# A routed mixture-of-experts block on one core: the late weight groups, the release of the output PSUM, the last block's halves and the last norm are rearranged

## The chip, the cores and the metric

The kernel runs on 1 core of one Trainium2 chip. The metric is the device time of one execution in microseconds, median of the runs shown. A profiled execution gives the trace.

## The reference

`x` has 16 batches of 256 rows of 256, the context 16 batches of 120 rows. What is computed, cut to what matters:

```python
x = x + xattn(layernorm(x), ctx, ctx)             # one head, softmax over 120 keys
h = layernorm(x)
logits = h @ Wr.T + br                            # 8 experts, the best 2 with softmax weights
for e in range(8):
    y = gelu(h @ W1[e].T + b1[e], approximate=False) @ W2[e].T + b2[e]     # 256 -> 1024 -> 256
    out = out + cw[:, e, None] * y
z = out + h
z = (z - mean(z)) * rsqrt(var(z) + 1e-12) * ln_w + ln_b
return x + z
```

## The kernel before, in words

Every engine has its own hand-written program; semaphores hold them together. The order of the work is therefore the order in which each engine's block calls its functions.

*First part (0 to about 184 us).* `steps` runs 16 batches, each taken through attention, routing and seat assignment in a pipeline of steps. Beside this the expert weights are turned: `transpose_group` (PE, L780) transposes four 128x128 tiles of `stage` into one of two PSUM banks `b_w`, `high_part` (ACT, L998) writes their high fp16 half, `low_part` (DVE, L1161) the rest. There are 64 such groups; PE may turn group n once n - 1 low parts are done (`wlo_ready`). The last 16 are late: eight of them run inside the last steps, and `late_groups(do, first, end)` calls the last eight, all of them W2, after the steps. All of W1 is done at `wlo_ready` = 56, everything at 64.

*Table.* After the steps DVE makes, from the counts in `b_rank` and the seats in `b_seats` (PSUM, last written by the matmuls L874), a list of 39 blocks of up to 256 rows: L1271 to L1321, with four small matmul steps of PE in between (L883 to L890, `table_ready`, `table_mm`). `blocks_ready` (L1317) says that expert and row of each block are known.

*Blocks.* For each block POOL's `fetch(m, p)` loads two registers, copies the indices (L633), starts a gather for each tile of 128 rows (L638) and copies the bias. PE's `turn` transposes the rows (L901), ACT's `x_high` (L1071) and DVE's `x_low` (L1328) split them into two fp16 parts, `up` does 48 matmuls (L922 to L924, four quarters in the PSUM banks 0 to 3), ACT's `gelu` (L1081) and DVE's `split` (L1337, L1339) make the two halves of h, and `down` does 48 matmuls (L944 to L946) into the banks 5 and 6, tile by tile within each of eight column parts. `y_out` on DVE evicts the two tiles (L1347), adds the norm's bias to a half batch of x1 (L1352) and multiplies by the gates (L1356), after which `y_ready` is raised. POOL's `give` copies the target indices (L650), once the earlier scatters have landed, waits for `y_ready` and scatters with addition into DRAM (L654). PE runs `up` of block j+1, `down` of j, `up` of j+2, `down` of j+1, and a `down` waits for `y_ready` of the block before:

```python
                j = 2 * m + p
                later = None
                at_least(pe, y_ready, j)
```

For the last block `up` lies before the previous block's `down`, so nothing is left to PE between the two.

*Early rows.* From m = 11 on, each pair of blocks also finishes a batch whose rows are complete: `measure_early` (DVE), `norm_early` (POOL), `normal_early` (ACT), `weigh_early` (POOL, L675), `finish_early` (DVE, L1387), which stands on DVE ahead of `y_out(m, 1)`.

*Last norm.* When all scatters have landed, SP loads the last eight batches; `measure_z` (DVE, L1421, L1425), `norm_pair` (POOL, L709 to L715), `normal` (ACT, L1121), `weigh` (POOL, L719; the last one DVE, L1440), `finish` (DVE, L1431) and `store` (ACT's queue, L1127) follow, two batches at a time. All of it is in place in `z_all`, in SBUF.

## Time and profile before

| what | us |
|---|---|
| median of 3 runs (663.43 to 664.11) | 664.06 |
| the profiled execution | 661.07 |
| its span | 659.4 |
| PE busy | 567.7 (86%) |
| DVE busy | 434.5 (66%) |
| ACT busy | 281.5 (43%) |
| POOL busy | 332.1 (50%) |
| DVE's block list finished (L1317, 192.99 + 0.17) | 193.16 |
| mean granted clock of TensorE | 0.938 of 2.4 GHz |

Times in the trace run from the span's start. A row of a timeline gives start, duration, engine, line, operation, written and read tiles, count, and in brackets how long the engine had been idle and what released it. In a row of stages each engine has its busy time and number of instructions; then come the clock (1.00 is 2.4 GHz, 0.50 is 1.2 GHz), the busy share of the DMA engines and GB/s. Matmuls are pipelined: their durations overlap, and their starts tell the pace.

### The profile page before, as it was taken

To read this page: it belongs to the slowest core of one execution; us is meant where nothing else is said; L and a number is where in the kernel's file an instruction comes from. 1 tells how busy PE (TensorE), PEld (TensorE's weight loads), DVE (VectorE), ACT (ScalarE), POOL (GpSimd) and SP (SyncE) were. 2 spreads that over 40 slices of the span, in tenths; PEclk is the share of its full clock that TensorE was granted. 3 is DMA by queue.
4 is the path that set the end of the run, shared out by engine and by line. 5 is a ranking of instruction groups with operands and counts; after the bars stand their busy time and mean duration, and the time that the engine had idled before them with its cause. 6 is when DMAs were issued, how large, how long until landed. Compare 5 with 4: busy or idle time off the path is not lost. (4 is left out here: it accounts for less than half of the span.)

```text
span 659.4 us, 17771 instructions
## 1 busy us (share of the span) xinstructions
PE 567.7 (86%) x4878; PEld 497.2 (75%) x4879; DVE 434.5 (66%) x1365; ACT 281.5 (43%) x699; POOL 332.1 (50%) x527
## 2 busy tenths in 40 slices
PE   5999888989647999998999999999999999999400
PEld 4888787887536887777989898988888898888300
DVE  2579988899874575446575656575667576666445
ACT  2687767666324333333333333325332433443022
POOL 4024433344313345544566666666766666665356
PEclk9999999888668999999999999999999999999855
DMA  7365665456432134332334342433434343443253
GB/s 217 100 190 194 187 208 170 156 168 197 126 93 55 35 50 62 58 66 55 58 59 64 57 64 57 64 73 76 85 74 91 68 82 88 89 80 59 41 144 127
DMA packets 62403, 65.71 MB, mean 100 GB/s; under 512 B 10088, under 2 KB 58032, under 8 KB 62352
## 3 DMA queue, kind: packets, MB, share of 16 engines
q1 hardware_dynamic: 46544, 44.10, 22.2%
q0 software_dynamic: 13632, 18.91, 18.6%
q10 hardware_dynamic: 2176, 2.10, 0.9%
q8 instruction: 22, 0.36, 0.2%
q14 instruction: 29, 0.24, 0.1%
HBM read 43.07 MB, written 22.02 MB: 99 GB/s over the span
## 5 line engine op out<-in xcount | busy, mean ns | idle before, releaser
L1081 ACT ACTIVATE stage<-bank,mt 128x256 f32<-128x256 f32 (+1 forms) x312 | 121.9, 452 | 138.9 <-PE bank L924 135.0
L922 PE MATMUL bank<-xnt,w1hi 128*128 128x256 f16 (+1 forms) x624 | 164.0, 264 | 9.0 <-DVE xnt L1328 5.5
L654 POOL DMA_INDIRECT sums_dram<-xn,mt x71 | 114.7, 1615 | 107.6 <-DVE xn L1356 89.9
L944 PE MATMUL bank<-w2hi,stage 128*128 x568 | 155.7, 274 | 10.9 <-DVE xn L1356 10.7
L923 PE MATMUL bank<-xnt,w1hi 128*128 128x256 f16 (+1 forms) x624 | 163.2, 263 | 0.0
L924 PE MATMUL bank<-xnt,w1lo 128*128 128x256 f16 (+1 forms) x624 | 163.2, 263 | 0.0
L946 PE MATMUL bank<-w2hi,stage 128*128 x568 | 155.5, 274 | 0.0
L945 PE MATMUL bank<-w2lo,stage 128*128 x568 | 155.5, 274 | 0.0
L1337 DVE CAST stage<-stage 128x512 f16<-128x512 f32 (+1 forms) x156 | 65.2, 418 | 115.0 <-PE bank L946 95.0
L638 POOL DMA_INDIRECT xg<-tokens_dram,mt x71 | 81.6, 1150 | 52.7 <-POOL mt L633 19.7
L1339 DVE TENSOR_TENSOR stage<-stage 128x512 f16<-128x512 f32 (+1 forms) x156 | 102.6, 657 | 5.4
L922 PEld LDWEIGHTS bank<-xnt,w1hi 128*128 x624 | 60.8, 97 | 22.6 <-issue 11.8
L944 PEld LDWEIGHTS bank<-w2hi,stage 128*128 128x128 f16 x568 | 55.7, 98 | 21.0 <-issue 14.9
L923 PEld LDWEIGHTS bank<-xnt,w1hi 128*128 x624 | 61.1, 98 | 5.8
L924 PEld LDWEIGHTS bank<-xnt,w1lo 128*128 x624 | 60.8, 97 | 6.1
L945 PEld LDWEIGHTS bank<-w2lo,stage 128*128 128x128 f16 x568 | 55.7, 98 | 6.6
L946 PEld LDWEIGHTS bank<-w2hi,stage 128*128 128x128 f16 x568 | 55.7, 98 | 6.5
L1071 ACT CAST xnt<-bank 128x512 f16<-128x512 f32 (+1 forms) x39 | 21.4, 548 | 67.2 <-PE bank L901 67.2
L780 PE MATMUL bank<-ident,stage 128*128 128x128 f32 x256 | 45.7, 314 | 4.2 <-DVE w2lo L1161 3.6
L586 POOL TENSOR_SCALAR nmu<-mv 128x4 f32<-128x4 f32 (+1 forms) x19 | 4.6, 242 | 88.6 <-DVE mv L1205 78.1
L780 PEld LDWEIGHTS bank<-ident,stage 128*128 128x128 f32 x256 | 36.0, 163 | 7.8 <-DVE w2lo L1161 3.5
L633 POOL COPY mt<-mt 128x2 int32 (+1 forms) x39 | 34.4, 883 | 5.9 <-DVE wvt L1321 4.8
(217 smaller groups left out, 915.4 us busy)
## 6 DMA issues: line engine op xcount, KB each, us to landing
stage<-in_L_ffn_W_dram SPq DMA_DIRECT2D x16, 768.0 KB, 4.9
work<-in_L_ffn_b_dram SPq DMA_DIRECT2D x39, 128.0 KB, 2.9
x<-in_x_dram SPq DMA_DIRECT2D x16, 256.0 KB, 5.1
tokens_dram<-xn SPq DMA_DIRECT2D x16, 256.0 KB, 2.2
sums_dram<-xn SPq DMA_DIRECT2D x16, 256.0 KB, 2.7
stage<-in_L_ffn_W_dram SPq DMA_DIRECT2D x16, 256.0 KB, 3.6
work<-sums_dram SPq DMA_DIRECT2D x8, 256.0 KB, 3.4
out_dram<-x SPq DMA_DIRECT2D x8, 256.0 KB, 3.2
```

The costliest lines, as they stand in the source:

```text
L638: nc.gpsimd.indirect_dma_start(out=xg[p][:, t, :], out_offset=None, in_=tokens_dram, in_offset=bass.IndirectOffsetOnAxis(ap=gidx[p][:, t:t ...
L654: nc.gpsimd.indirect_dma_start(out=sums_dram, out_offset=bass.IndirectOffsetOnAxis(ap=sidx[p][:, t:t + 1], axis=0), in_=y_sb[p][:, t, :], ...
L780: ins = nc.tensor.transpose(b_w[w][:, q * P:(q + 1) * P], stage[p][:, col:col + P], ident[:, :])
L922: nc.tensor.matmul(dst, w1hi[:, col], xhi[:, k, 0:bt], start=(k == 0), stop=False)
L923: nc.tensor.matmul(dst, w1hi[:, col], xlo[:, k, 0:bt], start=False, stop=False)
L924: ins = nc.tensor.matmul(dst, w1lo[:, col], xhi[:, k, 0:bt], start=False, stop=(k == KD - 1))
L944: nc.tensor.matmul(f_y[t], hhi[:, h], w2hi[:, col], start=(c == 0), stop=False)
L945: nc.tensor.matmul(f_y[t], hhi[:, h], w2lo[:, col], start=False, stop=False)
L946: ins = nc.tensor.matmul(f_y[t], hlo[:, h], w2hi[:, col], start=False, stop=(c == KF - 1))
L1081: ins = nc.scalar.activation(h32[:, c * bt:(c + 1) * bt], f_h[q][:, (c % 2) * bt:(c % 2 + 1) * bt], ACT.Gelu, bias=b1s[p][:, c:c + 1], sca ...
L1337: nc.vector.tensor_copy(hhi[:, s], h32[:, s]).then_inc(hhi_ready, 1)
L1339: nc.vector.tensor_tensor(hlo[:, s], h32[:, s], hhi[:, s], ALU.subtract).then_inc(split_ready, 1)
```

## The change

1. *Table and late groups.* DVE waits for the seats and makes the table before the low part of the group that the last step holds. PE turns one late group before the table's matmuls, three after them; the other four are turned inside `up` of block 0, one behind each quarter, and `up` needs only W1. `high_part` and `low_part` of these four go behind the four `gelu` and behind `x_low(0, 0)`. `fetch` reads the expert's register after its gathers are started.
2. *PSUM of outputs.* `down` waits for `y_self`, which the eviction raises. In `y_out` the gates are multiplied before the addition to x1.
3. *Last block.* `down` does all of tile 0, then all of tile 1. DVE evicts and multiplies each on its own, POOL scatters each on its own.
4. *Last norm.* `normal` writes into PSUM banks 0 to 7; DVE multiplies from there into `z_all`, POOL adds x1 (the last batch: DVE).

```diff
@@ fetch (POOL)
-                e = pool.value_load(eid[0:1, bass.ds(j, 1)], min_val=0, max_val=E - 1)
                 r = pool.value_load(row[0:1, bass.ds(j, 1)], min_val=0, max_val=UNITS - tb)
...
+                e = pool.value_load(eid[0:1, bass.ds(j, 1)], min_val=0, max_val=E - 1)
                 at_least(pool, gelu_ready, HB * (j - 1))
@@ give (POOL)
                 for t in range(tb):
+                    if isinstance(m, int) and j == BLOCKS - 1 and t > 0:
+                        alone(pool, y_ready, j + 1 + t, tally_pool)
@@ last norm (POOL)
-            def weigh(b):
...
+            def finish(b):
+                pool.wait_ge(zw_ready, b - ON_TIME + 1)
+                nc.gpsimd.tensor_tensor(z_all[:, b, :, :], z_all[:, b, :, :], x1[:, b, :, :], ALU.add).then_inc(o_ready, 1)
 
             norm_pair(0)
+            norm_pair(1)
+            for q in range(2, PAIRS):
                 norm_pair(q)
+                finish(ON_TIME + 2 * q - 4)
+                finish(ON_TIME + 2 * q - 3)
+            for b in range(NB - 4, NB - 1):
+                finish(b)
@@ PE
-            late_groups(transpose_group, 0, 2)
+            late_groups(transpose_group, 0, 1)
...
-            late_groups(transpose_group, 2, 8)
+            late_groups(transpose_group, 1, 4)
@@ up
                     if c % 2 == 1:
                         ins.then_inc(h_mm, 1)
+                        if beside is not None:
+                            beside(c // 2)
@@ down
-                at_least(pe, y_ready, j)
+                at_least(pe, y_self, j)
@@
             turn(0, 0)
+            pe.wait_ge(wlo_ready, GROUPS * NB + 4 * LATE - 8)
+            up(0, 0, weights_at(0, 0), (0, 1), beside=lambda q: late_groups(transpose_group, 4 + q, 5 + q))
+            turn(0, 1)
             pe.wait_ge(wlo_ready, GROUPS * NB + 4 * LATE)
@@ last block (PE)
-            down(LAST + 1, 0, weights_at(LAST + 1, 0))
+            at = weights_at(LAST + 1, 0)
+            j = BLOCKS - 1
+            pe.wait_ge(y_self, j)
+            pe.wait_ge(split_ready, HB * BLOCKS)
+            for t in range(TB):
+                for c in range(KF):
...
+                ins.then_inc(y_mm, HB // TB)
@@ ACT
-            ahead(0, 0, 0, 1)
+            for q in range(HB):
+                gelu(0, 0, q)
+                late_groups(high_part, 4 + q, 5 + q)
+            x_high(0, 1)
@@ normal (ACT)
-                    ins = nc.scalar.activation(z_all[:, b, j, :], z_all[:, b, j, :], ACT.Identity,
+                    ins = nc.scalar.activation(bank[b - ON_TIME][:, j * D:(j + 1) * D], z_all[:, b, j, :], ACT.Identity,
@@ step and table (DVE)
-                low_part(t, project, 3)
+                if not isinstance(t, int) or t < NB + 4:
+                    low_part(t, project, 3)
...
             dve.wait_ge(rank_kept, NB)
+            dve.wait_ge(seats_mm, NB)
...
-            late_groups(low_part, 0, 8)
+            low_part(NB + 4, None, 3)
+            late_groups(low_part, 0, 4)
@@ y_out (DVE): the gates' loop and its wait now stand ahead of this
                 if tiles(m, p) == TB:
@@ DVE
             keep_gate(0, 0)
+            late_groups(low_part, 4, 8)
             x_low(0, 1)
@@ last block (DVE)
-            y_out(BLOCKS // 2, 0)
...
+            for t in range(TB):
+                dve.wait_ge(y_mm, HB * last + HB // TB * (t + 1))
...
+                dve.wait_ge(y_self, last + t + 1)
@@ last norm (DVE)
-            def finish(b):
...
+            def weigh(b):
+                dve.wait_ge(zn_ready, b - ON_TIME + 1)
+                nc.vector.tensor_tensor(z_all[:, b, :, :], bank[b - ON_TIME][:, :].rearrange("p (j d) -> p j d", j=TJ),
+                                        lnw_bc[:, :].unsqueeze(1).to_broadcast([P, TJ, D]), ALU.mult).then_inc(zw_ready, 1)
```

PE's order from the seats to the table's last matmuls, before the change (L780 is `transpose_group`, four transposes of one group) and with it (L784):

```order
355 L874 MATMUL bank<-w2hi 128x256 [waits hot_ready]
356 L874 MATMUL bank<-w2hi 128x256 x3
357 L780 MATMUL bank<-ident,stage 128x128 [waits wlo_ready]
359 L780 MATMUL bank<-ident,stage 128x128 [waits wlo_ready,w_loaded0]
361 L780 MATMUL bank<-ident,stage 128x128 [waits wlo_ready]
363 L883 MATMUL bank<-work,before 128x2 [waits table_ready]
```

```order
355 L878 MATMUL bank<-w2hi 128x256 [waits hot_ready]
356 L878 MATMUL bank<-w2hi 128x256 x3
357 L784 MATMUL bank<-ident,stage 128x128 [waits wlo_ready]
359 L784 MATMUL bank<-ident,stage 128x128 [waits wlo_ready,w_loaded0]
361 L887 MATMUL bank<-work,before 128x2 [waits table_ready]
```

One group has moved behind the table's matmuls. Between these and `turn` stood six groups, now three.

DVE's order from the table's end to the second block's rows, before (L1161 is `low_part`, L1328 `x_low`) and with the change (L1185, L1354):

```order
405 L1321 TENSOR_TENSOR wvt<-work 128x272
406 L1161 SCALAR_TENSOR_TENSOR w2lo<-bank,w2hi 128x512 x8
407 L1328 TENSOR_TENSOR xnt<-bank,xnt 128x512
411 L1366 COPY mt<-xg 128x2
412 L1328 TENSOR_TENSOR xnt<-bank,xnt 128x512
```

```order
405 L1346 TENSOR_TENSOR wvt<-work 128x272
406 L1185 SCALAR_TENSOR_TENSOR w1lo<-bank,w1hi 128x512
407 L1185 SCALAR_TENSOR_TENSOR w2lo<-bank,w2hi 128x512 x4
408 L1354 TENSOR_TENSOR xnt<-bank,xnt 128x512
412 L1392 COPY mt<-xg 128x2
413 L1185 SCALAR_TENSOR_TENSOR w2lo<-bank,w2hi 128x512 x4
414 L1354 TENSOR_TENSOR xnt<-bank,xnt 128x512
```

Four low parts have moved between the first and the second `x_low`, and one of W1 from before the table to behind it.

POOL's order in the last norm, before (L719 multiplies by the weights) and with the change (L722 adds x1):

```order
674 L719 TENSOR_TENSOR w1hi<-w1hi,ctx_sb 128x512 x2
678 L715 TENSOR_TENSOR w1lo<-w1lo 128x4
679 L719 TENSOR_TENSOR w1hi<-w1hi,ctx_sb 128x512 x2
683 L715 TENSOR_TENSOR w1lo<-w1lo 128x4
684 L719 TENSOR_TENSOR w1hi<-w1hi,ctx_sb 128x512 x3
```

```order
677 L718 TENSOR_TENSOR w1lo<-w1lo 128x4
678 L722 TENSOR_TENSOR w1hi<-w1hi,x 128x512 x2
682 L718 TENSOR_TENSOR w1lo<-w1lo 128x4
683 L722 TENSOR_TENSOR w1hi<-w1hi,x 128x512 x5
```

POOL's seven operations of 512 columns stay seven, but begin after the third norm and are the last operation on each batch.

## Rows read from the trace of the kernel before

**Rows 1.** Stages: start:end, length, busy us (x count) of each engine, clock, DMA.
```profile
182.40:204.10 21.70, 10.10 (x47) 7.72 (x46) 14.97 (x53) 7.44 (x12) 5.50 (x11) 0.62 0.38 99
...
631.10:659.40 28.30, 0.00 (x0) 0.00 (x0) 16.11 (x41) 8.28 (x16) 17.30 (x23) 0.50 0.44 149
```

**Rows 2.** Timeline of DVE at the table: start, us, instruction [idle before <-releaser].
```profile
183.97 0.69 DVE L1161 SCALAR_TENSOR_TENSOR w1lo<-bank,w1hi 128x512 f16<-128x512 f32 x1 [2.01 <-ACT w1hi L998]
184.57 0.16 DVE L1271 COPY work<-bank 128x8 f32<-128x8 f32 x1
```

**Rows 3.** Timeline of PE from the last seats to block 1.
```profile
181.41 1.03 PE L874 MATMUL bank<-w2hi 128*128 128x256 f16 x4 [1.51 <-DVE w2hi L1224]
...
204.08 0.28 PE L922 MATMUL bank<-xnt,w1hi 128*128 128x256 f16 x1 [1.52 <-DVE xnt L1328]
...
209.33 0.60 PE L901 MATMUL bank<-ident,xg 128*128 128x128 f32 x4
211.70 0.28 PE L922 MATMUL bank<-xnt,w1hi 128*128 128x256 f16 x1 [1.77 <-DVE xnt L1328]
```

**Rows 4.** Timeline of POOL, the first index copy for a gather.
```profile
194.72 0.18 POOL L633 COPY mt<-mt 128x2 int32 x1 [4.81 <-DVE wvt L1321]
```

**Rows 5.** Stages of a quarter microsecond, PEclk before the busy share of DMA.
```profile
202.25:202.50 0.25, 0.25 (x2) 0.00 (x0) 0.11 (x1) 0.10 (x1) 0.00 (x0) 0.66 0.06 17
```

**Rows 6.** PE's waits in all (us, times, longest), then its timeline.
```profile
PE bank L944 <- DVE xn L1356: 10.7, 8, 5.0
...
457.81 0.28 PE L944 MATMUL bank<-w2hi,stage 128*128 x1 [0.72 <-DVE xn L1356]
...
616.13 0.39 PE L944 MATMUL bank<-w2hi,stage 128*128 x1 [5.02 <-DVE xn L1356]
...
618.67 0.37 PE L944 MATMUL bank<-w2hi,stage 128*128 x1
```

**Rows 7.** Timeline of DVE, then of POOL, one round with early rows.
```profile
501.52 0.75 DVE L1347 SCALAR_TENSOR_TENSOR xn<-bank,work 128x256 f32<-128x256 f32 x2
...
502.51 0.61 DVE L1356 TENSOR_SCALAR xn<-xn,mt 128x256 f32<-128x256 f32 x2
...
523.64 0.69 DVE L1387 TENSOR_TENSOR x<-x,work 128x512 f32<-128x512 f32 x1 [2.36 <-POOL work L675]
524.25 0.75 DVE L1347 SCALAR_TENSOR_TENSOR xn<-bank,work 128x256 f32<-128x256 f32 x2
...
503.97 1.63 POOL L654 DMA_INDIRECT sums_dram<-xn,mt  x1 [2.97 <-DVE xn L1356]
...
522.35 1.26 POOL L675 TENSOR_TENSOR work<-work,ctx_sb 128x512 f32<-128x512 f32 x1
```

**Rows 8.** Timeline of POOL, the scatters of the last two blocks.
```profile
618.67 1.56 POOL L654 DMA_INDIRECT sums_dram<-xn,mt  x1 [0.30 <-issue]
622.77 0.19 POOL L650 COPY mt<-wvt 128x2 int32 x1 [2.54 <-DMA sums_dram<-xn,mt]
...
627.22 1.55 POOL L654 DMA_INDIRECT sums_dram<-xn,mt  x1 [0.30 <-issue]
```

**Rows 9.** Timelines of POOL and of ACT's queue at the end, then four lines' durations.
```profile
635.76 0.25 POOL L709 TENSOR_SCALAR w1lo<-w1lo 128x4 f32<-128x4 f32 x1 [6.99 <-DVE w1lo L1425]
...
637.41 0.20 POOL L715 TENSOR_TENSOR w1lo<-w1lo 128x4 f32<-128x4 f32 x1
...
649.76 4.15 POOL L719 TENSOR_TENSOR w1hi<-w1hi,ctx_sb 128x512 f32<-128x512 f32 x3
...
654.49 2.19 ACTq L1127 DMA_DIRECT2D out_dram<-w1hi  x4
...
L1121 ACT ACTIVATE w1hi<-w1hi,w1lo x16: 585/586/602, 637.6 to 651.3; 128x256 f32<-128x256 f32 x16
L1431 DVE TENSOR_TENSOR w1hi<-w1hi,x x8: 677/679/1745, 640.9 to 655.6; 128x512 f32<-128x512 f32 x8
L1328 DVE TENSOR_TENSOR xnt<-bank,xnt x39: 417/683/694, 203.2 to 598.8; 128x512 f16<-128x512 f32 x32, 128x256 f16<-128x256 f32 x7
```

More of the change, by code:

```diff
@@ L359, in build @@
         o_ready = sem("o_ready")
+        last_done = sem("last_done")
         stored = sem("stored")
@@ L906, in weights_at, with up @@
                 return pe.value_load(woff[0:1, bass.ds(2 * m + p, 1)], min_val=0, max_val=(E - 1) * WE)
-            def up(m, p, at, after):
+            def up(m, p, at, after, beside=None):
                 j = 2 * m + p
@@ L1125, in store @@
             def store(b):
-                act.wait_ge(o_ready, b - ON_TIME + 1)
+                if b < NB - 1:
+                    act.wait_ge(o_ready, b - ON_TIME + 1)
+                else:
+                    act.wait_ge(last_done, 1)
                 act.dma_start(out_v[:, b, :, :], z_all[:, b, :, :]).then_inc(stored, 16)
@@ L1349, in y_out @@
                 ins.then_inc(y_self, 1)
+                dve.wait_ge(y_self, j + 1)
+                for t in range(tiles(m, p)):
+                    ins = nc.vector.tensor_scalar(y_sb[p][:, t, :], y_sb[p][:, t, :], gate_now[p][:, t:t + 1], None, ALU.mult)
+                ins.then_inc(y_ready, 1)
                 if tiles(m, p) == TB:
@@ L1353, in y_out @@
                                             x1[:, bass.ds(f, 1), half, :].rearrange("p a d -> p (a d)"), lnb_bc[:, :], ALU.add)
-                dve.wait_ge(y_self, j + 1)
-                for t in range(tiles(m, p)):
-                    ins = nc.vector.tensor_scalar(y_sb[p][:, t, :], y_sb[p][:, t, :], gate_now[p][:, t:t + 1], None, ALU.mult)
-                ins.then_inc(y_ready, 1)
                 if not (isinstance(m, int) and 2 * (m + 1) + p >= BLOCKS):
@@ L1413, in _ @@
                 blocks_of(m, m - ON_TIME_AT)
-            y_out(BLOCKS // 2, 0)
+            last = BLOCKS - 1
+            dve.wait_ge(b2_loaded[0], 16 * (last // 2 + 1))
+            dve.wait_ge(scattered[0], landed(last // 2, 0))
+            for t in range(TB):
+                dve.wait_ge(y_mm, HB * last + HB // TB * (t + 1))
+                nc.vector.scalar_tensor_tensor(out=y_sb[0][:, t, :], in0=f_y[t], scalar=1.0 / W_SCALE,
+                                               in1=b2_now[0], op0=ALU.mult, op1=ALU.add).then_inc(y_self, 1)
+                dve.wait_ge(y_self, last + t + 1)
+                nc.vector.tensor_scalar(y_sb[0][:, t, :], y_sb[0][:, t, :], gate_now[0][:, t:t + 1], None, ALU.mult).then_inc(y_ready, 1)
+            f = FULL - 1
+            nc.vector.tensor_tensor(x1[:, f // 2, f % 2, :], x1[:, f // 2, f % 2, :], lnb_bc[:, :], ALU.add)
             def measure_z(q):
@@ L1436, in _ @@
                 measure_z(q)
-                finish(ON_TIME + 2 * q - 4)
-                finish(ON_TIME + 2 * q - 3)
-            dve.wait_ge(zn_ready, NB - ON_TIME)
-            nc.vector.tensor_tensor(z_all[:, NB - 1, :, :], z_all[:, NB - 1, :, :],
-                                    lnw_bc[:, :].unsqueeze(1).to_broadcast([P, TJ, D]), ALU.mult).then_inc(z_self, 1)
-            for b in range(NB - 4, NB - 1):
-                finish(b)
-            dve.wait_ge(z_self, PAIRS + 1)
-            finish(NB - 1)
+                weigh(ON_TIME + 2 * q - 4)
+                weigh(ON_TIME + 2 * q - 3)
+            for b in range(NB - 4, NB):
+                weigh(b)
+            dve.wait_ge(zw_ready, NB - ON_TIME)
+            nc.vector.tensor_tensor(z_all[:, NB - 1, :, :], z_all[:, NB - 1, :, :], x1[:, NB - 1, :, :], ALU.add).then_inc(last_done, 1)
 _INS = ['x', 'ctx_1024', 'L0_xattn_Wq', 'L0_xattn_bq', 'L0_xattn_Wk', 'L0_xattn_bk', 'L0_xattn_Wv', 'L0_xattn_bv',
```

20 lines of the change are left out of this document (6 added, 14 removed).

## The prediction

> **What bounds the kernel now.** I read the table by stages first [rows 1]. TensorE (PE) is busy in almost all of the stage of blocks, and hardly at all in two places: the turn from routing to blocks (182.4 to 204.1 us: 10.1 of 21.7 us) and the final norm (631.1 to 659.4: nothing). In the first of them the order is: the seat matmuls L874, VectorE's (DVE) chain for the block table, GpSimd's (POOL) gathers, `turn`, `x_high`, `x_low`, and the first matmul of `up` at 204.08 [rows 2 to 4].
>
> Inside the blocks I read what PE waits for [rows 6]: 10.7 us on L1356, `y_ready`, in 8 waits. One is 5.0 us, before the last block; the other seven sum to 5.7 us, the first at 457.81 with 0.72. They lie in the rounds that also finish early rows. The timeline of one such round [rows 7] says why: POOL runs nearly without a gap from the scatter at 503.97 to the end of its weigh at 523.61, then DVE adds (523.64) and evicts the odd block (524.25), multiplies by the gates, and the next scatter may start. That circle lasts 524.25 - 501.52 = 22.73 us. PE's own work in it is 0.72 us less, so **POOL and DVE, not PE, set the pace of these rounds**.
>
> At the end [rows 8, 9] PE is done; what counts is the scatter that starts last (627.22), its landing, eight loads, and POOL's norms and multiplications, until 649.76 + 4.15 = 653.91; DVE's adds and ACT's last store issues follow, until 656.68.
>
> **The change, part by part.** A measurement here tells about 0.2%, 1.3 us.
>
> (a) *Table sooner.* DVE's chain starts at 184.57, behind a low part that waits for ScalarE (ACT) [rows 2]; it needs only the seat matmuls, over at 181.41 + 1.03 = 182.44 [rows 3]. It now starts near 182.5: 2.05 us sooner, the low part going behind it. POOL's first index copy starts at 194.72 [rows 4], after two register loads that I take at 0.7 us each (estimate: half of the 1.4 us between DVE's finished list, 193.16 in the table above, and that copy, with 0.15 for the start); one of them moves behind the gathers. The gathers so come up to 2.75 us sooner, and `turn` is no longer kept behind six groups of transposes but waits for its rows. Before: `turn` ended at 202.56, 1.52 us ahead of `up` [rows 3]. After: near 198.5, `up` near 200.1, some 4 us sooner.
>
> (b) *Four groups beside block 0.* They aren't gone. PE gets four times four transposes inside `up`, 0.45 us each time (estimate: the four of `turn` take 0.60 with the end of their pipeline [rows 3]), ACT four activations, DVE four low parts of 0.69 [rows 2], and `x_low(0,1)` is behind the last one. With PE at 2.4 GHz throughout, `up` of block 1 would start near 209.7 instead of 211.70 [rows 3]. But the granted clock rose to the upper level only at 202.3, in the dense stretch just ahead of `up` [rows 5]. Now `up` starts earlier and behind thinner work, so I expect its first matmuls at 1.2 GHz. The price is in the last block: 12 matmuls took 616.13 to 618.67, 0.212 us each [rows 6], against (211.70 - 204.08 - 1.77 - 0.60) / 48 = 0.109 us in block 0 [rows 3], where 0.60 is `turn`: 1.2 us. Gain at `up` of block 1: 2.0 - 1.2 = 0.8; I take **1.2 us** for the chance that it is warm sooner. Bounds: 0 (all given back) and 2.9. From there to 457 us PE is the bound, so it stays.
>
> (c) *PSUM free at eviction.* PE's wait ends with the eviction (`y_self`) and not with the gates. From 501.52 + 0.75 = 502.27 to 502.51 + 0.61 = 503.12 [rows 7] this is 0.85 us. Also the gates go ahead of the x1 add; the add is 0.33 us of chain, of which a dependent start takes back about 0.12, so `y_ready` comes 0.21 sooner. In the first of the eight rounds the wait of 0.72 vanishes. Then POOL's circle decides: 22.73 - 0.21 = 22.52 a round against PE's 22.01. After the six further rounds the next to last stop has gained 0.86 + 6 x 0.21 = **2.1 us**. Not 5.7: the waits get shorter, about 0.4 us each, they don't go. Bounds: 0.9 (only the wait's end moves) and 5.7 (all seven waits).
>
> (d) *Last block.* PE's 5.02 us wait gets 0.85 shorter, which buys nothing by itself: the new order has tile 0 finished 24 matmuls early, so POOL could scatter it early, but its index copy waits for the landing of block 37's scatter: 618.67 to 622.77 [rows 8], now 0.21 sooner. Then 622.56 + 0.19 + 0.85 = 623.6 for tile 0 (0.85 us is what a scatter takes to start, as from 503.12 to 503.97 [rows 7]), 1.57 + 0.30 later 625.5 for tile 1. Its data is there: PE restarts at 615.28 and ends 2.54 + 36 x 0.109 + 0.3 = 6.8 us later, near 622.1, DVE 0.9 after that. Today 627.22 [rows 8]: **1.7 us**. Bounds: 0.5, if a wait between the two scatters costs as much as today's 0.8 us before the first and the landing is slower, and 2.6.
>
> (e) *Final norm.* POOL has 4 norms of 1.85 (635.76 to 637.61) and 7 operations of 512 columns at 1.26 as before, but DVE multiplies out of PSUM, and POOL's additions are now the last step. POOL's serial chain: 635.76 + 4 x 1.85 + 7 x 1.26 = 652.0, plus 0.2 of waits and 0.4 of what the last three cost beside DVE (4.15 against 3.78) [rows 9]: 652.6. Two store issues of 0.44 end at 653.5; today the last four end at 656.68. Gain **3.1 us**. DVE's fourth measurement is no longer behind additions that waited for POOL, so nothing else is late: its multiplications end near 649.4. Cover: ACT writes into PSUM; no row shows such an activation; the nearest is L1121 itself, 0.586 [rows 9], and between half and one and a half of that, 16 of them stay ahead of POOL's 16.8 us. Bounds of (e): 0 and 4.
>
> DVE's multiplication with a PSUM input: L1328 has one, median 683 ns for 512 columns; L1431 has none, 679 alone [rows 9]. I take 0.68. The Trainium skill, "VectorE: DVE Perf Modes", section "The TRN2 errata — SBUF-src ops pay a fixed extra latency per instruction", speaks against the change: it gives a PSUM source 62 cycles more, an estimated 0.065 us at its 0.96 GHz. By that rule (e) would lose at most 8 x 0.065 = 0.5 us; by these rows nothing.
>
> **Sum:** 1.2 + 2.1 + 1.7 + 3.1 = 8.1 us. The profiled span 659.4 becomes 651.3. The profiled execution took 661.07, 1.7 more than its span; the median of the runs is 664.06, 3.0 above that. I take the gain off the median: **656.0 us**.
>
> **Rivals.**
> 1. *DVE and POOL still hinder each other in the norm.* L1431 took up to 1745 ns beside POOL, 677 alone [rows 9]: both have their inputs in SBUF. Now DVE has one input in PSUM and one in SBUF. If one is enough to collide, each of seven multiplications costs POOL up to 0.44 us, and gain (e) goes: 656.0 + 3.1 = 659.1. For: DVE's own weight row is still in SBUF. Against: L1328, with just such inputs, has a median of 683 and a maximum of 694 ns in the whole trace, POOL busy or not.
> 2. *The waits all go.* If POOL's gap-free stretch has slack that I don't see, (c) gives 5.7: 652.4. Against: [rows 7].
> 3. *The start gives nothing.* If the gates' store, and not the table, holds the gathers, or the clock stays low a little longer, (a) and (b) cancel: 657.2.
> 4. *Slower: the clock stays low.* PE starts `up` at 1.2 GHz with transposes and waits mixed in, and does not rise. Each matmul at the lower level costs 0.212 - 0.109 = 0.103 us. It takes (8.1 + 1.3) / 0.103 = 91 of them to make the kernel slower; through `up` 0, `up` 1 and `down` 0 (144) it is 14.8, of which (b) holds 1.2 already: about 656.0 + 14.8 - 1.2 = 669.6. Against: in the last block it rose after 12 matmuls.
>
> **Chances.** Forecast 0.70; rival 1 0.11; rival 2 0.06; rival 3 0.10; rival 4 0.03. All but the last, and a corner of 1 with 3 together, are faster by over 1.3 us: 0.94 faster, 0.03 same, 0.03 slower. The range holds rivals 1 and 3, and the low end takes (b) at 2.5 and (c) at 3 and (e) at 3.5: 653.0 to 660.0.
>
> **What would show it.** Start of the table chain near 182.5; first `up` near 200 at the lower clock, `up` of block 1 near 210.5 to 211; rounds of 22.5 us with a wait of 0.4 us on the eviction; last scatter to first scatter 1.9 us apart, released by no DVE row; POOL without a gap from the first norm to its last add, DVE's multiplications all below 0.7 us. A last add of POOL before 648 or after 651 us (652.6 less the 5.0 gained ahead of it is 647.6; a miss of 3) would make (e) wrong, an interval between odd evictions of 22.0 or 22.7 would make (c) wrong.

## The result and the profile after

| | before | changed |
|---|---|---|
| median of the runs (lowest to highest), us | 663.74 (660.65 to 664.11, 4 runs) | 652.88 (651.9 to 653.17, 4 runs) |
| profiled execution: time, span, us | 661.07, 659.4 | 651.9, 650.1 |
| granted TensorE clock, mean | 0.938 | 0.933 |

The changed kernel takes 0.9847 of the time before, 95% interval 0.9824 to 0.9871: 10.1 us less (8.6 to 11.7). The ratio weighs all runs and isn't the quotient of the two medians, which lie 10.9 apart; the gains of the parts alone, below, are taken from ratios too, differences between two changed kernels from medians. The forecast was 8.1 less. 652.88 lies just below the low end of the range, 653.0; the ratio applied to the 664.06 that the forecast started from gives 653.9, inside it.

The table chain and the first two blocks, timelines of DVE, then of PE, of the changed kernel, against [rows 2 and 3]:

```profile
179.84 0.17 DVE L1297 COPY work<-bank 128x8 f32<-128x8 f32 x1 [0.60 <-PE bank L878]
...
178.70 1.03 PE L878 MATMUL bank<-w2hi 128*128 128x256 f16 x4 [1.48 <-DVE w2hi L1248]
...
195.28 1.09 PE L905 MATMUL bank<-ident,xg 128*128 128x128 f32 x4 [1.60 <-DMA xg<-tokens_dram,mt]
197.85 0.39 PE L926 MATMUL bank<-xnt,w1hi 128*128 128x256 f16 x1 [1.48 <-DVE xnt L1354]
...
209.09 0.28 PE L926 MATMUL bank<-xnt,w1hi 128*128 128x256 f16 x1 [2.11 <-DVE xnt L1354]
```

Everything already stands 2.71 us earlier at the last seat matmuls (181.41 before, 178.70 now), in code that the change doesn't touch. So times are read from the seats, that is, from the start of the last four seat matmuls (L874, now L878). The table starts 0.11 us behind them, as forecast; `up` of block 0 comes 19.15 us behind them instead of 22.67; but `up` of block 1 comes 30.39 behind, where it was 30.29. The reason is in the stages of 1 us of the changed kernel, PEclk before the busy share of DMA:

```profile
199.00:200.00 1.00, 1.00 (x7) 0.69 (x6) 0.00 (x0) 0.00 (x0) 0.95 (x1) 0.50 0.00 0
200.00:201.00 1.00, 1.00 (x6) 0.94 (x5) 0.00 (x0) 0.37 (x2) 0.70 (x2) 0.50 0.27 55
201.00:202.00 1.00, 1.00 (x11) 0.91 (x10) 0.02 (x1) 0.95 (x3) 0.27 (x1) 0.98 0.29 97
```

`up` runs at 1.2 GHz for 3.2 us. The waits of PE in the blocks, then the last two on the timeline, against [rows 6]; the last line is the kernel before's counterpart of the first of these two:

```profile
PE bank L986 <- DVE xn L1373: 4.2, 1, 4.2
PE bank L950 <- DVE xn L1373: 3.8, 6, 1.6
...
590.07 0.28 PE L950 MATMUL bank<-w2hi,stage 128*128 x1 [0.44 <-DVE xn L1373]
610.56 0.35 PE L986 MATMUL bank<-w2hi,stage 128*128 x1 [4.16 <-DVE xn L1373]
...
594.79 0.28 PE L944 MATMUL bank<-w2hi,stage 128*128 x1 [0.74 <-DVE xn L1356]
```

Two evictions of odd blocks are 520.72 - 498.27 = 22.45 us apart (22.73 in [rows 7]), and POOL's multiplication (L678) is still what DVE waits for last ahead of them. DVE's timeline of the changed kernel:

```profile
498.27 0.75 DVE L1373 SCALAR_TENSOR_TENSOR xn<-bank,work 128x256 f32<-128x256 f32 x2
...
520.11 0.69 DVE L1413 TENSOR_TENSOR x<-x,work 128x512 f32<-128x512 f32 x1 [2.93 <-POOL work L678]
520.72 0.75 DVE L1373 SCALAR_TENSOR_TENSOR xn<-bank,work 128x256 f32<-128x256 f32 x2
```

The last block and the norm, POOL's timeline, ACT's queue, and two lines' durations (min/median/max), against [rows 8, 9]:

```profile
617.79 0.18 POOL L651 COPY mt<-wvt 128x2 int32 x1 [2.49 <-DMA sums_dram<-xn,mt]
...
620.67 1.55 POOL L657 DMA_INDIRECT sums_dram<-xn,mt  x1 [0.30 <-issue]
629.26 0.25 POOL L712 TENSOR_SCALAR w1lo<-w1lo 128x4 f32<-128x4 f32 x1 [7.04 <-DVE w1lo L1462]
...
639.03 6.59 POOL L722 TENSOR_TENSOR w1hi<-w1hi,x 128x512 f32<-128x512 f32 x5
...
641.55 5.01 ACTq L1151 DMA_DIRECT2D out_dram<-w1hi  x5
...
L1467 DVE TENSOR_TENSOR w1hi<-bank,ctx_sb x8: 656/680/692, 632.8 to 641.8; 128x512 f32<-128x512 f32 x8
L722 POOL TENSOR_TENSOR w1hi<-w1hi,x x7: 1255/1264/1710, 634.8 to 644.4; 128x512 f32<-128x512 f32 x7
```

Of POOL's seven adds one takes 1.71 us, the others 1.26. That one lies beside DVE's add of the last batch (L1479), the one operation of DVE there that has both inputs in SBUF.

In this pair of profiles the 9.3 us of the span are: setup and routing 2.7, which is not the change's; start of the blocks -0.1 (30.29 - 30.39); rounds 2.1 (594.79 - 590.07, less the 2.61 that `up` of block 1 had gained); last block 1.8 (627.22 - 620.67 = 6.55, less 4.72); norm 2.7 and 0.1 of rounding and loads. **The profiles give the change 6.5 us, the medians 10.1.** The experiments are about both numbers.

### The profile page after: what moved, and what is told of

It reads as the page before. It is cut to its first block, busy times and chain, and to the rows that moved or that the text cites. A ratio compares the mean times of both kernels' runs of the same rounds, so it can differ in the third digit from the quotient of the medians.

```text
span 650.1 us, 17773 instructions
## 1 busy us (share of the span) xinstructions
PE 564.9 (87%) x4878; PEld 496.0 (76%) x4879; DVE 431.6 (66%) x1365; ACT 279.5 (43%) x699; POOL 319.6 (49%) x527
## 4 chain that ended last, share of the span: by engine, by line
PE 43%; POOL 15%; issue 15%; DVE 11%; DMA 3%; POOLq 3%; ACT 2%; DVEq 1%; SPq 0%; ACTq 0%
PE bank L926 7%; PE bank L928 6%; PE bank L927 6%; PE bank L950 6%; PE bank L952 5%; PE bank L951 5%; POOL sums_dram L657 5%; POOL xg L638 2%; DVE st L1214 2%; PE bank L784 2%; PE bank L905 1%; POOL work L678 1%; POOL rn L590 1%; PE bank L865 1%; POOL w1hi L722 1%
## 5 line engine op out<-in xcount | busy, mean ns | idle before, releaser
L950 PE MATMUL bank<-w2hi,stage 128*128 x552 | 150.6, 273 | 4.0 <-DVE xn L1373 3.8
L951 PE MATMUL bank<-w2lo,stage 128*128 x552 | 150.5, 273 | 0.0
L952 PE MATMUL bank<-w2hi,stage 128*128 x552 | 150.5, 273 | 0.0
L638 POOL DMA_INDIRECT xg<-tokens_dram,mt x71 | 74.7, 1052 | 51.6 <-POOL mt L633 26.7
L950 PEld LDWEIGHTS bank<-w2hi,stage 128*128 128x128 f16 x552 | 53.9, 98 | 13.3 <-issue 7.5
L951 PEld LDWEIGHTS bank<-w2lo,stage 128*128 128x128 f16 x552 | 54.0, 98 | 6.1
L952 PEld LDWEIGHTS bank<-w2hi,stage 128*128 128x128 f16 x552 | 54.0, 98 | 6.0
L784 PE MATMUL bank<-ident,stage 128*128 128x128 f32 x256 | 44.6, 306 | 3.0 <-DVE w1lo L1185 2.4
L784 PEld LDWEIGHTS bank<-ident,stage 128*128 128x128 f32 x256 | 35.4, 160 | 5.6 <-DVE w1lo L1185 2.5
L633 POOL COPY mt<-mt 128x2 int32 (+1 forms) x39 | 31.1, 798 | 2.9 <-DVE wvt L1346 2.4
```

What stands on the lines that cost most here:

```text
L638: nc.gpsimd.indirect_dma_start(out=xg[p][:, t, :], out_offset=None, in_=tokens_dram, in_offset=bass.IndirectOffsetOnAxis(ap=gidx[p][:, t:t ...
L784: ins = nc.tensor.transpose(b_w[w][:, q * P:(q + 1) * P], stage[p][:, col:col + P], ident[:, :])
L950: nc.tensor.matmul(f_y[t], hhi[:, h], w2hi[:, col], start=(c == 0), stop=False)
L951: nc.tensor.matmul(f_y[t], hhi[:, h], w2lo[:, col], start=False, stop=False)
L952: ins = nc.tensor.matmul(f_y[t], hlo[:, h], w2hi[:, col], start=False, stop=(c == KF - 1))
```

## The experiments

All times that follow are medians beside runs of the kernel before on the same chip (its medians there: 662.9 to 663.6). The changed kernel itself was not run again beside them, so differences between these kernels and 652.88 under about 2 us are not told apart from none.

### The parts alone

**Only (e), the norm.** Of the change, this alone:

```diff
-                    ins = nc.scalar.activation(z_all[:, b, j, :], z_all[:, b, j, :], ACT.Identity,
+                    ins = nc.scalar.activation(bank[b - ON_TIME][:, j * D:(j + 1) * D], z_all[:, b, j, :], ACT.Identity,
```

with `weigh` on DVE and `finish` on POOL.

> The kernel before with the new last norm alone. Theory A (each part has a gain of its own, and 2.7 us of the 9.3 between the two profiled spans arose before the table, where nothing was changed): from the first load of the norm (28.3 us before the end of the span, 25.6 with the whole change) 25.6, so 2.7 us faster than before. Theory B (DVE and POOL still collide with one input of DVE in SBUF): POOL's seven additions stretch to 1.7 us each and the stretch stays at 28 us. First table of rows to look at: DVE's eight multiplications, 0.68 us each by A, up to 1.7 by B.

Measured: 659.55, ratio 0.9954 (0.9939 to 0.9968), 3.1 us less. From the first load of sums to the end it took 25.7 us, before 28.3.

**Only (c) and (d), release and halves.**

```diff
-                at_least(pe, y_ready, j)
+                at_least(pe, y_self, j)
```

with the gates ahead of the x1 add, and the last `down` tile by tile.

> The kernel before with the wait on the eviction, the gates ahead of the x1 addition, and the last block by halves; start and norm as before. Theory A: rounds of 22.5 us with waits of 0.45 us on the eviction, none in the first; last scatter 1.8 us sooner relative to the last block: 3.9 us faster. Rival (the 2.1 us of the rounds depend on the earlier start): waits of 0.7 us stay, 1.8 us faster.

Measured: 658.02, ratio 0.9912 (0.9895 to 0.993), 5.8 us less (4.6 to 7.0). The rounds are the changed kernel's, with waits of 0.45.

**Only (a) and (b), the start.**

```diff
-            up(0, 0, weights_at(0, 0), (0, 1))
+            up(0, 0, weights_at(0, 0), (0, 1), beside=lambda q: late_groups(transpose_group, 4 + q, 5 + q))
```

with the sooner table and gathers.

> The kernel before with the sooner table and the four late groups beside block 0 alone. Theory A: the shift of 2.6 us at the start of block 1 between the two profiles came from the setup, where narrow fp32 matmuls took 0.13 us each instead of 0.23; from the first of the last seat matmuls to the first matmul of block 1 it stays 30.3 us, and the kernel is 0 to 0.5 us faster than before. Theory C (the start itself gives the 2.6): that stretch is 27.7 us in this run and it is 2.6 us faster.

Measured: 661.43, ratio 0.9979 (0.9963 to 0.9994), 1.4 us less. `up` of block 1 starts 30.35 us behind the seats, so nothing is gained there by this profile. This profile also has two stretches of 1.2 GHz in the blocks, behind a wait of 2.00 us at 307 us and behind one of 2.15 us at 549.5.

The three ratios multiply to 0.9954 x 0.9912 x 0.9979 = 0.9846, and the whole change has 0.9847: within these intervals the parts don't disturb or help each other.

### The start: four groups beside block 0, and TensorE's clock

The level is TensorE's granted clock, 1.2 or 2.4 GHz; a fall is its change from 2.4 to 1.2. A fill is a row of matmuls on constants, placed where TensorE would wait; nothing reads what they write.

**The groups back ahead of block 0**, the sooner table kept:

```diff
-            late_groups(transpose_group, 1, 4)
+            late_groups(transpose_group, 1, 8)
```

> The changed kernel with all late groups turned before block 0 again, the table still sooner. Theory A: the sooner table pays by itself: up of block 0 starts after 7 groups of transposes that begin 2.0 us sooner than before, so from the last seat matmuls to block 1 it takes 28.3 us or less, and the four groups beside a slow block 0 cost what they gain: this kernel is 1 to 2 us faster than the changed one. Theory D (the groups beside block 0 pay as meant): 1 to 2 us slower than the changed kernel.

Measured: 653.77, ratio 0.9859 (0.9842 to 0.9876); intervals overlap with the changed kernel's, so neither theory's 1 to 2 us is borne out. Three timelines of PE, the last seats, the two `up`: this kernel, then the one with only (e), then the one with (c) and (d). The last two have the old start unchanged.

```profile
178.67 1.03 PE L878 MATMUL bank<-w2hi 128*128 128x256 f16 x4 [1.47 <-DVE w2hi L1242]
...
201.55 0.39 PE L926 MATMUL bank<-xnt,w1hi 128*128 128x256 f16 x1 [1.50 <-DVE xnt L1348]
...
210.67 0.28 PE L926 MATMUL bank<-xnt,w1hi 128*128 128x256 f16 x1 [1.78 <-DVE xnt L1348]
```
```profile
180.23 1.04 PE L876 MATMUL bank<-w2hi 128*128 128x256 f16 x4 [1.52 <-DVE w2hi L1229]
202.94 0.39 PE L924 MATMUL bank<-xnt,w1hi 128*128 128x256 f16 x1 [1.51 <-DVE xnt L1333]
...
212.24 0.28 PE L924 MATMUL bank<-xnt,w1hi 128*128 128x256 f16 x1 [1.78 <-DVE xnt L1333]
```
```profile
180.88 1.03 PE L876 MATMUL bank<-w2hi 128*128 128x256 f16 x4 [1.47 <-DVE w2hi L1237]
203.59 0.28 PE L924 MATMUL bank<-xnt,w1hi 128*128 128x256 f16 x1 [1.52 <-DVE xnt L1341]
...
211.21 0.28 PE L924 MATMUL bank<-xnt,w1hi 128*128 128x256 f16 x1 [1.78 <-DVE xnt L1341]
```

A first matmul of 0.39 is one at 1.2 GHz, 0.28 one at 2.4. The same start code gave both: 9.30 us between the two `up` at the lower level, 7.62 at the upper, so 1.7 us hang on a level that differs from one execution to the next. Seen from the seats, `up` of block 1 comes after 32.0 us (both kernels that began low without groups beside), 30.3 (high), and 30.3 to 30.5 with the groups beside block 0, which began low each time in the seven profiles without constant matmuls ahead of it. The sooner table alone moves nothing: `up` of block 0 comes 22.88 us behind the seats with it and 22.71 without. With the groups beside it, block 0 takes 11.24 us between the two `up`, without them 9.12: they cost 2.1 and save 3.7.

**TensorE busy ahead of the setup's matmuls.**

```diff
+            pe.wait_ge(pool_self, 1)
+            for i in range(34):
+                nc.tensor.matmul(bank[6][:, 0:P], ones_bf[:, :], ones_bf[:, :], start=True, stop=True)
```

> The changed kernel, with 34 bf16 128x128 matmuls of a constant into an unused PSUM bank while TensorE waits for the first weights; nothing reads them. Theory A (what the setup gains from run to run is TensorE's clock at the fp32 matmuls of one column: 1.05, 1.03 and 0.58 us for 8, 8 and 4 in one profile, 1.87, 1.84 and 0.99 in another, the same code): with the engine busy ahead of them they take 1.05, 1.03 and 0.58 us, the first V is evicted near 17.8 us, and the time is 0 to 2 us below that of the changed kernel, 651 to 653 us. Theory B (the difference comes from elsewhere, a transfer or a wait): they keep either time whatever ran before, and the time is 652.9 us or some tenths above, by what the extra matmuls delay.

Measured: 653.23, ratio 0.9862 (0.9834 to 0.989): not to be told from the changed kernel. This is the setup's first group of narrow matmuls in this kernel, and in the kernel of the run with two filled waits, below, which has that code as in the kernel before. Below them stand two stages of 1 us within that group, of the kernel before and of the changed one:

```profile
9.20 1.05 PE L759 MATMUL bank<-bqk,w2lo 128*128 128x1 f32 x8 [0.32 <-DVE w2hi L1179]
```
```profile
11.16 1.86 PE L756 MATMUL bank<-bqk,w2lo 128*128 128x1 f32 x8
```
```profile
11.00:12.00 1.00, 1.00 (x6) 1.00 (x6) 0.00 (x0) 0.20 (x2) 0.85 (x3) 1.00 1.10 351
11.00:12.00 1.00, 1.00 (x12) 1.00 (x11) 0.00 (x0) 0.04 (x1) 0.92 (x2) 1.00 1.12 356
```

Of 12 profiles without this fill (with before and after) eight show 1.05 to 1.08 and four 1.86 to 1.87; the last seats came at 178.4 to 179.5 us in the former and at 180.2 to 181.8 in the latter. The kernels before, only (e), and (c) with (d) were of the latter, the changed one of the former. The stages show 6 matmuls in a microsecond against 12 and a clock of 1.00 in both, so that this is TensorE's clock is not shown. Nor is it shown that it is a toss: it was slow in all three profiles of kernels without the sooner table, and in one of the nine with it. Both profiles with the fill have the fast one, which eight of twelve have without it. The fill brought this group 1.3 us forward against the changed kernel (9.20 against 10.51) and the seats to 178.1; the median doesn't show it.

**TensorE busy ahead of `up` of block 0**, then **also ahead of `up` of block 1** (the last two lines):

```diff
+            for _ in range(20):
+                nc.tensor.matmul(bank[3][:, 0:P], ones_bf[:, :], ones_bf[:, :], start=True, stop=True)
             late_groups(transpose_group, 1, 4)
...
             turn(0, 1)
+            for _ in range(28):
+                nc.tensor.matmul(bank[7][:, 0:P], ones_bf[:, :], ones_bf[:, :], start=True, stop=True)
```

> The changed kernel, with constant bf16 128x128 matmuls in TensorE's idle stretches ahead of the first block: 20 behind the block list, 18 behind the late groups that come before the block, 11 behind its turn. Nothing reads them. Theory A (the changed start gains nothing because up of block 0 begins at 1.2 GHz: 0.213 us per matmul for its first 3 us): up of block 0 starts at 2.4 GHz, 0.107 us per matmul, up of block 1 starts 28.7 to 29.3 us behind the last seat matmuls, where the changed kernel has 30.4, and the time is 1.1 to 1.7 us below that of the changed kernel, near 651.5. Theory B (what follows up of block 0 waits for something else, the gather of block 1 or the splits of the late groups): up of block 0 is shorter, but up of block 1 stays at 30.4 and the time at 652.9. Theory C (the extra matmuls delay the late groups or the turn more than they save): over 653.5.

Measured: 653.54, ratio 0.9855 (0.9825 to 0.9885). `up` of block 0 began at 2.4 GHz and `up` of block 1 28.15 us behind the seats, 2.2 us sooner than in the changed kernel. Then it was given back. PE's timeline of this kernel:

```profile
207.62 0.28 PE L930 MATMUL bank<-xnt,w1hi 128*128 128x256 f16 x1 [2.11 <-DVE xnt L1360]
...
208.94 0.39 PE L930 MATMUL bank<-xnt,w1hi 128*128 128x256 f16 x1
209.13 0.42 PE L931 MATMUL bank<-xnt,w1hi 128*128 128x256 f16 x1
```

Behind the wait of 2.11 us the level fell, at 208.9, and rose again at 212.2. The same wait, of 2.10 to 2.20 us, had no fall behind it in the seven other profiles that have it. None of the three theories had this.

> The changed kernel with constant matmuls ahead of the first block as in the run before (20, 18 and 11), and 28 more in the 2.1 us that TensorE waits between the turn of block 1 and its up, in another bank. Theory A (the first warm start was given back because the granted clock fell to 1.2 GHz behind that wait, from 208.9 to 212.2 us, 16 matmuls at 0.213 us): with the wait filled the clock stays at 2.4 GHz through up of block 1, the Fori's first wait (296.6 in the changed kernel, seats + 117.9) comes 1.8 to 2.3 us sooner relative to the last seat matmuls, and the time is 1.5 to 2.3 us below that of the changed kernel, near 651. Theory B (the clock falls somewhere later in the block, whatever fills the first waits): the same 653 to 653.6 as with the first warm start.

Measured: 650.94, ratio 0.9826 (0.9795 to 0.9857), six runs from 648.64 to 655.38. That is 1.9 us below the changed kernel, as theory A has it, but the intervals overlap. The wait was down to 0.58 and the level stayed. The profiled run is one of the long ones: slow setup (above), and another fall, behind a wait of 2.00 us ahead of `up` of block 12:

```profile
308.00:309.00 1.00, 0.33 (x2) 0.26 (x3) 0.97 (x3) 0.00 (x0) 0.00 (x0) 0.87 0.00 0
309.00:310.00 1.00, 1.00 (x7) 0.68 (x5) 0.97 (x3) 0.00 (x0) 0.00 (x0) 0.50 0.00 0
310.00:312.00 2.00, 2.00 (x11) 1.38 (x10) 1.49 (x4) 0.57 (x2) 0.00 (x0) 0.50 0.00 0
```

From that `up` to the wait near 478 us it is 171.31 us here and 169.64 in the changed kernel's profile, which has no fall there: 1.7 us. The wait of 2.00 us ahead of block 12 is in all 13 profiles in which it isn't filled, the fall in 7 of them.

### The rounds

**Gates behind the x1 add again**, PSUM still free at the eviction:

```diff
-                for t in range(tiles(m, p)):
-                    ins = nc.vector.tensor_scalar(y_sb[p][:, t, :], ..., gate_now[p][:, t:t + 1], None, ALU.mult)
-                ins.then_inc(y_ready, 1)
                 if tiles(m, p) == TB:
                     ...
+                (the same lines here)
```

> The changed kernel with one thing put back: VectorE multiplies a block's outputs by their gates behind the x split of the block that follows, and not at once behind the eviction. PSUM is still free at the eviction. Theory A (with PSUM free at the eviction, the rounds are set by the circle of the gates, the scatter and the index copies of VectorE and GpSimd): gates that come later make the scatters later, the rounds go from 22.45 us to 22.6 to 22.7 and the last ones with them; 1.0 to 1.7 us slower than the changed kernel, 653.9 to 654.6. Theory B (the release of PSUM alone is worth the gain; the order of the gates doesn't matter, since the scatter has a whole round to land): rounds of 22.45 us and 652.6 to 653.2.

(The gates stood behind the x1 add, not behind the x split as the expectation says; the place is that of the kernel before.)

Measured: 660.78, ratio 0.997 (0.9948 to 0.9992); one more execution took 1292.4 us, for no reason that the runs show. 7.9 us slower than the changed kernel, many times what both theories said. PE's waits, two evictions of odd blocks on DVE, and POOL's timeline at a round's first scatters:

```profile
PE bank L950 <- DVE xn L1373: 9.7, 6, 1.6
...
502.41 0.74 DVE L1373 SCALAR_TENSOR_TENSOR xn<-bank,work 128x256 f32<-128x256 f32 x2
526.06 0.75 DVE L1373 SCALAR_TENSOR_TENSOR xn<-bank,work 128x256 f32<-128x256 f32 x2
```
```profile
504.85 1.63 POOL L657 DMA_INDIRECT sums_dram<-xn,mt  x1 [2.97 <-DVE xn L1382]
506.79 2.08 POOL L657 DMA_INDIRECT sums_dram<-xn,mt  x1 [0.30 <-issue]
508.31 1.04 POOL L633 COPY mt<-mt 128x2 int32 x1
```

and the same three in the changed kernel:

```profile
500.51 1.63 POOL L657 DMA_INDIRECT sums_dram<-xn,mt  x1 [2.76 <-DVE xn L1378]
502.45 1.56 POOL L657 DMA_INDIRECT sums_dram<-xn,mt  x1 [0.30 <-issue]
503.46 0.80 POOL L633 COPY mt<-mt 128x2 int32 x1
```

Rounds are 23.65 us, 1.2 more than in the changed kernel and 0.9 more than in the kernel before, which has the same order but the later release. The later gates are 0.2 us of the 1.2; the rest goes with POOL being slower at the same work: from 470 to 590 us its scatters take 1.87 us in the mean, in the changed kernel 1.65, its index copies 1.20 and 0.93. They now lie at other places beside DVE's instructions. Beside the scatter of 2.08 us is this one of `split`'s casts, which elsewhere take 0.43:

```profile
507.95 0.65 DVE L1363 CAST stage<-stage 128x512 f16<-128x512 f32 x1
```

So the two seem to hinder each other, as DVE and POOL do in [rows 9]. This is the likeliest reading and not shown: scatters of 1.56 us have such casts beside them too, and no run moved one.

**TensorE waits for the gates again**, the gates still first:

```diff
-                at_least(pe, y_self, j)
+                at_least(pe, y_ready, j)
```

> The changed kernel with the other half of its part on PSUM undone: TensorE waits for the gates (the count behind the multiplication) and not for the eviction, but the gates still stand ahead of the x1 add. So it keeps what the run with gates last gave up, and gives up what that one kept. Theory A (GpSimd's circle sets the rounds, and what makes it short is that gates and scatter come early): rounds of 22.45 us as in the changed kernel, TensorE's wait in them 0.9 to 1.2 us in place of 0.45 and paid once, at the last of them; 0 to 0.9 us slower than the changed kernel, 652.9 to 653.8. Theory B (TensorE that starts later shifts VectorE's splits against GpSimd's scatters and makes them collide, as the run with gates last showed: scatters of 1.87 us in place of 1.65): rounds of 22.7 to 23.7 us and 654.5 to 661.

Measured: 653.8, ratio 0.9874 (0.9851 to 0.9898), 0.9 us over the changed kernel, which is within the noise. Rounds of 22.54 us with waits of 0.53. So the order of gates and add is nearly all of part (c): 22.73 to 22.54 by it, 22.54 to 22.45 by the earlier release; and the release without the order is a loss (rounds of 23.65 against 22.73).

**The early rows' multiplication on DVE.**

```diff
-                pool.wait_ge(early_zn, i + 1)
-                nc.gpsimd.tensor_tensor(z_now[i % 2], z_now[i % 2], lnw_bc..., ALU.mult).then_inc(early_zw, 1)
...
+                dve.wait_ge(early_zn, i + 1)
+                nc.vector.tensor_tensor(z_now[i % 2], z_now[i % 2], lnw_bc..., ALU.mult).then_inc(early_zw, 1)
                 dve.wait_ge(early_zw, i + 1)
```

> The changed kernel with one operation moved, in the rounds that also finish early rows: the multiplication of 512 columns by the norm's weight goes from GpSimd (1.26 us a round) to VectorE, just ahead of the add that waited for it. Theory A (GpSimd's circle of 22.45 us is what is left between the rounds and TensorE's 22.0): GpSimd has 1.26 us less, the circle opens, TensorE's seven waits of 0.45 us go, the one near 545 (1.3 to 1.6 us in most profiles) shrinks, rounds are 22.0 us; VectorE has 2.7 us of idle time in the round and takes the 0.7 us without being late; 2.5 to 4 us faster than the changed kernel, 649 to 650.4. Theory B (the multiplication lies on VectorE's path to the eviction): the waits stay at 0.3 to 0.5 us, and the time within 0.7 us of 652.9.

Measured: 648.5, ratio 0.9794 (0.9767 to 0.9821), 4.4 us below the changed kernel. PE's waits from 440 to 620 us, and a round on DVE:

```profile
PE bank L978 <- DVE xn L1365: 3.4, 1, 3.4
```
```profile
517.89 0.72 DVE L1405 TENSOR_TENSOR work<-work,ctx_sb 128x512 f32<-128x512 f32 x1
518.64 0.69 DVE L1408 TENSOR_TENSOR x<-x,work 128x512 f32<-128x512 f32 x1
519.25 0.75 DVE L1365 SCALAR_TENSOR_TENSOR xn<-bank,work 128x256 f32<-128x256 f32 x2
...
541.08 0.75 DVE L1365 SCALAR_TENSOR_TENSOR xn<-bank,work 128x256 f32<-128x256 f32 x2
```

Rounds of 21.83 us, and only the wait ahead of the last block is left. 21.83 us is also what two blocks take in the profiles before the early rows begin. GpSimd's circle was the bound.

### The norm

**The intermediate back in SBUF**, all else as changed:

```diff
-                    ins = nc.scalar.activation(bank[b - ON_TIME][:, j * D:(j + 1) * D], z_all[:, b, j, :], ACT.Identity,
+                    ins = nc.scalar.activation(z_all[:, b, j, :], z_all[:, b, j, :], ACT.Identity,
```

> The changed kernel with the final norm's intermediate back in SBUF: ScalarE writes its normalised rows in place, and VectorE multiplies SBUF by SBUF, at the same places of the program. Theory A (PSUM as one input is what takes the collision of VectorE and GpSimd away): VectorE's multiplications that run beside a GpSimd add take 1.2 to 1.75 us in place of 0.69, those adds end later, and the time from the first load of sums to the end goes from 25.6 to between 26.8 and 28.3 us; 1.2 to 2.7 us slower than the changed kernel, 654.1 to 655.6. Theory B (the gain is the order and the engines that the work was given to, not the memory): multiplications stay near 0.7 us, and the time stays within 0.5 us of 652.9.

Measured: 657.27, ratio 0.9913 (0.9882 to 0.9944), 4.4 us over the changed kernel. The two lines' durations here, where the changed kernel has 680 and 1264 in the median:

```profile
L1467 DVE TENSOR_TENSOR w1hi<-w1hi,ctx_sb x8: 658/688/1754, 634.9 to 646.7; 128x512 f32<-128x512 f32 x8
L722 POOL TENSOR_TENSOR w1hi<-w1hi,x x7: 1255/1708/1798, 637.8 to 650.1; 128x512 f32<-128x512 f32 x7
```

Five of the seven adds now take 1.70 to 1.80 us, in the changed kernel one; their sum is 11.2 us against 9.3, 1.9 longer. Counted from the first load, the first add also starts 1.1 us later, and the fourth norm, between the adds, takes 0.8 longer. From the first load to the end it is 29.5 us, 3.9 over the changed kernel's 25.6 and more than the 28.3 before: in these profiles the new order of the norm without PSUM is a loss.

### All of it together

The changed kernel with the multiplication on DVE, the fills of the runs above, and 28 constant matmuls ahead of `up` of block 12:

```diff
+                if isinstance(m, int) and m == SETTLED - 1:
+                    for _ in range(28):
+                        nc.tensor.matmul(bank[7][:, 0:P], ones_bf[:, :], ones_bf[:, :], start=True, stop=True)
                 at = up(m + 1, 0, at, (m, 1))
```

> The changed kernel with the multiplication of the early rows on VectorE (as in the run before, 648.5 us) and TensorE's waits filled with constant matmuls: 34 ahead of the first weights, 20, 18 and 11 ahead of block 0, 28 ahead of block 1, and 28 ahead of up of block 12, which waits 2.00 us at 307 us in all profiles and began at 1.2 GHz or fell to it within 4 us in 6 of the 11 profiles of changed kernels. Theory A (each such fall costs 1.7 us and the runs differ by which of them happen; the fill excludes them at these places): 1.5 us from the start as in the run that filled two waits, and 0.5 to 1.7 us from the wait at 307 us, so 644.5 to 647 us, with first-to-last spread below 2 us, where the run with the multiplication moved had 4.6. Theory B (the fill only moves the falls to other places): 647.5 to 649, spread as before.

(The count in it was wrong: the fall near 307 us was in 7 of the 13 profiles, the kernel before's with them.)

Measured: **646.65**, ratio 0.9749 (0.9729 to 0.9769), six runs from 645.2 to 647.56: the fastest of the study, 1.85 below the run with the multiplication alone, whose interval it just touches, and 6.2 below the changed kernel. The size is as theory A says; that the fills give it is likely and no more. In its profile the level stays up through the waits at 209.6 and 307.9, now 0.56 and 0.43. But the gather of block 0 came late (turn behind a wait of 2.18), the fill ahead of it ran out, and `up` of block 0 began at 1.2 GHz. The spread is 2.4 us, not below 2 as expected.

## Why the prediction was right, and where not

- **What bounds the kernel: right.** GpSimd's circle set the rounds; with 1.26 us taken from it, the waits of the rounds, seven before and six in the changed kernel, all went.
- **(a), sooner table: right in size** (3.5 us at `up` of block 0, forecast 4; `turn` waits 1.6 us for the gather to land), but it needs (b): without the four groups moved away nothing comes of it. **(b) was mis-sized.** The forecast let the groups cost 2.0 us (four times 0.45, and its own 209.7 has 0.2 more) and the lower clock 1.2: 0.8, rounded up to 1.2 "for the chance that it is warm sooner". They measured 2.1 and 1.5 to 1.7, and the profile gives -0.1, with 0.5 of (a) missing. That chance was the wrong way to round. More important, [rows 5] showed the clock rise just ahead of `up` in one execution, and the step took it as a property of the old start; the old start began high in two of three profiles and low in the third, and then loses it too (32.0 us). Against that the new start is 1.6 us sooner, which fits the 1.4 that the part alone gave, though the profiles can't tell how often each level comes, nor whether part of the 1.4 lies in the setup, which was slow with the old start in three of three profiles.
- **(c): right, 2.1 against 2.1** in the profiles (1.2 of it by the second wait, forecast 0.86 + 0.21, where the rows give 0.85 for the 0.86; 0.9 in the five rounds after it, forecast 1.05), and a round of 22.45 against 22.52, by the mechanism named (the gates' order 0.19 a round, forecast 0.21). What the step didn't see is that its first half, the release, alone would have cost 3.5 us or so (an estimate: 660.78 against 657.3, which is 663.6 less the 1.4, 1.8 and 3.1 of the other parts).
- **(d): right**, 1.8 against 1.7; the scatters are 1.86 apart, and no DVE row releases the second. The first's row does name DVE (L1449), but that multiplication of tile 0, at 615.62, had long ended when the index copy did at 617.97; the 0.83 us between copy and scatter are the forecast's 0.85.
- **(e): right**, 3.1 in the part alone, 2.7 in the profile: the last issue came 3.5 sooner against the loads (forecast 3.1), but its store landed later, so that 3.6 us lie behind the last issue where it was 2.7. POOL's chain from its first norm to its last add took 16.4 us, forecast 16.8. The forecast's sign for (e) being wrong, a last add before 648, did come, at 645.6; but the window of 648 to 651 leaves out the forecast's own 647.6, and with the 2.7 us of the setup and the 3.8 that (a) to (d) gave, the same sum has 646.1. Rival 1's collision is real, 0.44 us an add where it comes, and one PSUM input takes it away: with one, DVE's eight multiplications took 656 to 692 ns and six of POOL's adds 1.26 us. By the Trainium skill ("VectorE: DVE Perf Modes", section "The TRN2 errata — SBUF-src ops pay a fixed extra latency per instruction") a PSUM source would cost an estimated 0.065 us more an instruction. The rows don't show it: where nothing collided, multiplications with both inputs in SBUF took 658 to 691 ns.
- **Rivals 2 and 4 didn't come**: waits of 0.45 us stayed, and the clock rose after 3.2 us. Rival 3 is what the profiles show and what the medians don't. The low end of the range, 653.0, isn't the sum of its own terms either, 2.5 + 3 + 1.7 + 3.5, which gives 653.4.
- **The sum: the median moved 2.0 us more than forecast, the profile 1.6 less.** The forecast of 8.1 lies between 6.5 and 10.1, so that it came as near as it did is in part luck: (b) was 1.3 too high, and something that it didn't have gave more than that. The failed step is "I take the gain off the median". It supposes that the profiled execution and the median differ by the same in both kernels. Before, the median was 2.7 us above the profiled time, after 1.0; and the two profiles also differ by 2.7 us ahead of the change. Both differences have the size of what comes and goes between profiles, 1.7 to 2 us each, at five places: the setup's narrow matmuls, where the clock isn't shown to be the cause, and four places where the clock is low in some profiles and not in others, at `up` of block 0, behind the wait ahead of `up` of block 1, behind the one at 307 us and once behind one at 549.5. The excess is in the run of (c) and (d), 5.8 against a forecast of 3.8. **Why an unchanged setup is slow less often with the new start, and whether this is all of the excess, stays open**: only profiled executions show where the clock fell, and the mean clock of the others doesn't sort the times (in the kernel before 0.934 stands beside 664 and 0.931 beside 661).

## What to carry to other kernels

Where an engine waits a few tenths of a microsecond in every round, look for the engine whose row has no gap, and take work off it or put its releaser first; a buffer that comes free sooner is worth only what that circle lets through, and can be a loss if it moves two engines' instructions onto each other. VectorE and GpSimd, where both work on 512 columns out of SBUF, can be parted by letting VectorE read one input from PSUM. A profile shows one execution: before a level of the clock in it is made a term, look whether the same code shows it in a second profile.

## What was unexpected of the hardware

- The granted clock falls to 1.2 GHz behind single waits of about 2 us, at once or up to 1.3 us into the dense work that follows, in some executions and not in others (7 of 13 profiles at 307 us, 1 of 8 ahead of `up` of block 1), and cost 1.7 us where it was measured. Constant matmuls in the wait kept it up in the profiles in which they reached to its end.
- Eight fp32 matmuls of one column take 1.05 us in some executions and 1.86 in others, with a granted clock of 1.00 in the rows of both.
- GpSimd's issue of an indirect scatter, which has no arithmetic, took 1.56 to 2.08 us, most likely by what DVE did meanwhile.
